# Attention stage rewritten: scores in fours into four banks, one shared bank used in written order, value sums normalised with VectorE's 32x32 transposes

## The reference, cut to what matters

```
q, k: 8 heads of 64;  v: 8 heads of 16           (xl = layernorm(x))
dots = q k^T / 8;  bias[h, i, j] depends on j - i only
attn = softmax(dots + bias);  out = (attn v) W_out + b_out;  x = x + out
```

## Time and profile before

| | us |
|---|---|
| median of 3 runs | 1186.83 (1186.79 to 1189.51) |
| profiled execution, its time | 1184.94 |
| its span | 1183.1 |
| one batch of attention (batches 1 to 6) | 56.63 |

### The profile page before, as it was taken

One profiled execution on the slowest core, in us unless ns is written; L12 is line 12 of the kernel. 1 busy time (PEld: TensorE's weight loads), 2 busy tenths in 40 slices (PEclk: granted clock), 3 DMA queues, 4 the chain that ended last, 5 costly groups with the idle time before them and its releaser, 6 DMA issues. The chain is left out here.

```text
span 1183.1 us, 23592 instructions
## 1 busy us (share of the span) xinstructions
PE 1072.6 (91%) x7860; PEld 794.2 (67%) x7860; DVE 895.0 (76%) x1941; ACT 831.8 (70%) x1727; POOL 515.3 (44%) x321
## 2 busy tenths in 40 slices
PE   3876499999999999989969999999999999997897
PEld 3442389899899899769954454545454555556897
DVE  7697988989889889747737586868686868675565
ACT  4897798898898988546636675757575757672565
POOL 0288788898998998635520001010101010011354
PEclk9898599999999999989989999999999999998999
DMA  3000355555785685233320000000000000002331
GB/s 95 4 2 9 86 142 139 138 146 150 189 254 165 175 228 159 75 112 104 110 61 28 1 2 19 1 19 2 19 1 19 1 19 10 10 19 60 102 98 50
DMA packets 107670, 89.50 MB, mean 76 GB/s; under 512 B 35703, under 2 KB 85628, under 8 KB 107552
## 3 DMA queue, kind: packets, MB, share of 16 engines
q1 hardware_dynamic: 98672, 66.01, 21.0%
q0 software_dynamic: 5568, 12.66, 3.0%
q10 hardware_dynamic: 3312, 9.33, 2.7%
HBM read 71.49 MB, written 17.39 MB: 75 GB/s over the span
## 5 line engine op out<-in xcount | busy, mean ns | idle before, releaser
L1041 DVE TENSOR_TENSOR_SCAN h<-d_a,p_dbu 128x1024 f32<-128x1024 f32 x128 | 289.5, 2278 | 31.5 <-ACT d_a L792 26.8
L738 POOL TENSOR_TENSOR h<-h,c_rep 128x1024 f32<-128x1024 f32 x126 | 295.1, 2368 | 27.2 <-DVE h L1041 26.1
L1369 POOL DMA_INDIRECT expert_rows<-r_row,r_dest x60 | 59.5, 991 | 468.4 <-DVEq L1264 453.7
L2017 ACT ACTIVATE arena<-arena,at_min 128x512 f32<-128x512 f32 x256 | 182.3, 720 | 96.4 <-DVE at_min L2127 93.7
L2127 DVE CUSTOM_DVE_ANT_0 arena<-at_p_scores,arena 128x512 f32<-128x512 f32 x256 | 174.2, 684 | 59.3 <-PE at_p_scores L1885 57.3
L792 ACT ACTIVATE d_a<-arena,a_exp 128x511 f32<-128x511 f32 x256 | 168.0, 710 | 19.1 <-DVE h L1041 19.0
L1892 PEld LDWEIGHTS at_p_probs_T<-ident,arena 128*128 128x128 f32 x1024 | 111.8, 141 | 91.8 <-issue 64.1
L1885 PE MATMUL at_p_scores<-arena,at_q_T 64*128 64x512 f32 x512 | 159.3, 641 | 1.5 <-DVE arena L2115 1.5
L1892 PE MATMUL at_p_probs_T<-ident,arena 128*128 128x128 f32 x1024 | 157.4, 281 | 1.8 <-ACT arena L2017 1.2
L931 PE MATMUL p_y_T<-ident,h 128*128 128x128 f32 x1024 | 132.5, 273 | 1.2 <-DVE h L1096 1.1
L784 ACT ACTIVATE b_du_T<-arena,b_T 128x256 f32<-128x256 f32 x304 | 128.8, 496 | 0.0
(11 more groups left out here) (263 smaller groups left out, 1618.0 us busy)
## 6 DMA issues: line engine op xcount, KB each, us to landing
c_rep<-c_rows SPq DMA_DIRECT2D x128, 256.0 KB, 3.6
diag_b<-diag_rows SPq DMA_DIRECT2D x52, 256.0 KB, 4.1
f_row<-expert_rows SPq DMA_DIRECT2D x78, 129.0 KB
arena<-in_w_all ACTq DMA_DIRECT2D x8, 578.0 KB, 5.4
arena<-bias_by_distance ACTq DMA_DIRECT2D x8, 448.0 KB, 5.0
x_tok<-in_x SPq DMA_DIRECT2D x4, 512.0 KB, 6.1
x_tok<-x_between SPq DMA_DIRECT2D x8, 256.0 KB, 2.7
diag_rows<-diag_b SPq DMA_DIRECT2D x4, 256.0 KB, 3.0
```

What stands on the lines that cost most here:

```text
L738: nc.gpsimd.tensor_tensor(h[:, n % HS, :, :], h[:, n % HS, :, :], cc, ALU.mult).then_inc(prod_done, 1)
L1041: nc.vector.tensor_tensor_scan(h[:, n % HS, :, :].rearrange("p c t -> p (c t)"), da[:, s % 2, :, :].rearrange("p c t -> p (c t)"), p_dbu[: ...
L2017: nc.scalar.activation(pr[:, slot, :], sc[:, slot, :], ACT.Exp, scale=-1.0, bias=mn[:, slot:slot + 1]).then_inc(probs_ready, 1)
```

## The change

- `psc` has four banks. Scores are issued in fours (`quad`), one quad ahead of its turns: heads alternate between the two halves of the array as before.
- A batch is 8 parts. In part p (n = 8b + p) TensorE does: quad n+1; half of a value sum (`values(n-2)`); slot A; turns 4n, 4n+1, 4n+2; slot B; turn 4n+3. VectorE does: `begin`, four biases, take 4n, take 4n+2, `extras`. ScalarE does: three exponentials, slot A's copy, the fourth, take 4n+1, slot B's copy, take 4n+3.
- `pmm` is one bank. The work in slots A and B uses it in written order; each waits for the reader of the one before. All copies of projections go to ScalarE, k1, k2, k3 and v too (but k0 and k1 of batch 0).
- The value sums are no longer copied, transposed back, normalised, transposed again and copied. VectorE transposes `pot` in 32x32 blocks, takes reciprocals, multiplies, and transposes in blocks again. W_out is spread over two zero-filled 128-row tables (8 small DMAs and a memset in expert layer 1), and the output takes 8 products in place of 4.
- The ring of probabilities has 7 tiles in place of 4. The prologue spreads batch 0's projections over all free banks.
- The router's stages, LayerNorm and the residual sum are lumped into `begin` and `extras`.

```diff
-        self.w_qk, self.w_v, self.w_o, self.b_o = k.take(2 * H * DQK), k.take(D), k.take(D), k.take(D)
+        self.w_qk, self.w_v, self.w_o, self.b_o = k.take(2 * H * DQK), k.take(D), k.take(2, D), k.take(D)
...
+        sp.wait_ge(self.filled, 3)
+        for hd in range(H):
+            gr, q = hd // 4, hd % 4
+            sp.dma_start(self.w_o[32 * q:32 * q + DV, gr, :], self.k.dram["w_o"][hd * DV:(hd + 1) * DV, :]
+                         ).then_inc(self.w_in, 16)
...
-        psc = k.ps("at_p_scores", [P, SCB, T], ctx=c)
+        psc = k.ps("at_p_scores", [P, 4, T], ctx=c)
-        pmm = k.ps("at_p_mm", [P, 2, T], ctx=c)
+        pmm = k.ps("at_p_mm", [P, T], ctx=c)
+        AT_A = {0: "X", 1: "k0", 2: "k1", 3: "q2", 4: "R", 5: "q3", 7: "V"}
+        AT_B = {0: "q0", 1: "q1", 2: "O", 3: "k2", 4: "L", 5: "N", 6: "k3"}
...
+            def output(b):
+                pe.wait_ge(normed, (b + 1) * NG)
+                for j in range(TPB):
+                    for gr in range(NG):
+                        mm = nc.tensor.matmul(pmm[:, j * P:(j + 1) * P], onT[gr][:, j * P:(j + 1) * P],
+                                              w_o[:, gr, :], start=gr == 0, stop=gr == NG - 1)
+                mm.then_inc(o_done, 1)
...
+            def quad(n):
...
+                for g in range(4 * n, 4 * n + 4):
+                    if g >= 4:
+                        pe.wait_ge(biased, g - 4 + 1)
...
+                    nc.tensor.matmul(psc[:, g % 4, :], qT[b % 2][half, hd // 2, it * P:(it + 1) * P],
+                                     kT[b % 2][half, hd // 2, :], start=True, stop=True).then_inc(scored, 1)
...
+            for n in range(B * QUADS):
+                b, part = divmod(n, QUADS)
+                if n + 1 < B * QUADS:
+                    quad(n + 1)
+                if n >= 2:
+                    values(n - 2)
+                slot(b, AT_A.get(part))
+                for g in range(4 * n, 4 * n + 3):
+                    turn(g)
+                slot(b, AT_B.get(part))
+                turn(4 * n + 3)
...
+            def norm(b, gr, parts):
+                n = b * NG + gr
+                if 0 in parts:
+                    dve.wait_ge(valued, 2 * n + 2)
+                    dve.wait_ge(norm_step, 2 * n)
+                    V.transpose(o_tok.rearrange("p n e -> p (n e)"), pot[:]).then_inc(pot_free, 1)
+                    dve.wait_ge(pot_free, n + 1)
+                    V.reciprocal(rden[:], o_tok[:, :, DV]).then_inc(norm_step, 1)
+                    dve.wait_ge(norm_step, 2 * n + 1)
+                    dve.wait_ge(normed, n)
+                    V.tensor_tensor(o_normed, o_tok, rden[:].unsqueeze(2).to_broadcast([P, T // 32, 32]),
+                                    ALU.mult).then_inc(norm_step, 1)
+                if 1 in parts:
+                    dve.wait_ge(norm_step, 2 * n + 2)
+                    if b > 0:
+                        dve.wait_ge(o_done, b)
+                    V.transpose(onT[gr], o_norm).then_inc(normed, 1)
+            def begin(b, part):
+                if b > 0 and part == 3:
+                    route(b - 1, 1, 2)
+                elif b > 0 and part == 6:
+                    route(b - 1, 8, 9, 10, 11)
+            def extras(b, part):
+                if part == 0 and b + 2 < B:
+                    stats_of(b + 2)
+                elif part == 1 and b > 0:
+                    norm(b - 1, 1, (0, 1))
+                elif part == 2 and b > 0:
+                    add(b - 1)
+                    route(b - 1, 0)
+                elif part == 3 and b > 0:
+                    route(b - 1, 3)
+                elif part == 4 and b > 0:
+                    route(b - 1, 4, 5, 6, 7)
+                elif part == 5:
+                    norm(b, 0, (0,))
+                elif part == 6:
+                    norm(b, 0, (1,))
+                elif part == 7 and b + 2 < B:
+                    normalise(b + 2)
+            for n in range(B * QUADS):
+                b, part = divmod(n, QUADS)
+                begin(b, part)
+                if n + 1 < B * QUADS:
+                    for g in range(4 * n + 4, 4 * n + 8):
+                        bias(g)
+                take(4 * n)
+                take(4 * n + 2)
+                extras(b, part)
```

More of the change, by code:

```diff
@@ L1898, in _, with values @@
[L1898 to L1912, removed]
+            def values(i):
+                vg, part = divmod(i, 2)
+                b = vg * VS // ST
+                hd0, gr, _, it = head_of(vg * VS)
+                if part == 0:
+                    for e in range(2):
+                        pe.wait_ge(turned_taken[e], (vg + 1) * (VS // 2))
+                    if vg % 2 == 0:
+                        pe.wait_ge(proj_taken, taken(b, "V"))
+                        if vg > 0:
+                            pe.wait_ge(pot_free, vg // 2)
+                for j in range(TPB // 2 * part, TPB // 2 * (part + 1)):
@@ L1952, in core @@
-            def core(b, par, first, last):
-                for s in range(ST):
-                    if s % 2 == 0 and s + 2 < ST:
-                        scores(b, par, s + 2)
-                    elif s % 2 == 0 and not last:
-                        scores(b + 1, 1 - par, s + 2 - ST)
-                    if s in VALUES_AT:
-                        values(b, par, *VALUES_AT[s])
-                    if not first:
-                        tail(b, par, s)
-                    elif s + LATE < ST:
-                        head(-1, s + LATE)
-                    turn(b, s)
-                    if not last:
-                        head(b, s)
@@ new lines, in _ @@
+            bank_free[0] = (proj_taken, taken(0, "V"))
+            for n in range(B * QUADS):
[9 more added lines that the diff above has]
+                turn(4 * n + 3)
+            for i in range(B * QUADS - 2, B * QUADS):
+                values(i)
@@ new lines, in _ @@
+            rstds(1, None)
+            take_projected(0, "q0", ppt[:, 0, :])
+            take_projected(0, "q1", pot[:])
+            for g, u, bank in ((0, "q2", pmm), (1, "k2", pot), (2, "q3", pmm), (3, "k3", pot)):
+                take_projected(0, u, bank[:])
+                exp(g)
+            take_projected(0, "V", pmm[:])
+            for n in range(B * QUADS):
+                b, part = divmod(n, QUADS)
+                more = n + 1 < B * QUADS
+                if more:
+                    for g in range(4 * n + 4, 4 * n + 7):
+                        exp(g)
+                slot(b, AT_A.get(part))
+                if more:
+                    exp(4 * n + 7)
+                take(4 * n + 1)
+                if part == 3:
+                    rstds(b + 2 if b + 2 < B else None, b - 1 if b > 0 else None) if b + 2 < B or b > 0 else None
+                elif part == 5 and b > 0:
+                    rt.act_exps(act, b - 1)
+                    rt.act_rows(act, b - 1)
+                slot(b, AT_B.get(part))
+                take(4 * n + 3)
@@ L2163, in core @@
-            def core(b, par, first, last):
-                for s in range(ST):
-                    bias(b, s)
-                    if s >= 2 and s % 2 == 0:
-                        take(b, s - 2)
-                    if not first:
-                        tail(b, s)
-                    elif s + LATE < ST:
-                        head(-1, 0, s + LATE)
-                    if not last:
-                        head(b, 1 - par, s)
-            for s in range(LATE):
-                head(-1, 0, s)
@@ new lines, in _ @@
+            stats_of(0)
+            normalise(0)
+            stats_of(1)
+            take_k(0, ppt[:, 1, :])
+            take_k(1, pmm[:])
+            for g in range(4):
+                bias(g)
+            normalise(1)
+            for n in range(B * QUADS):
+                b, part = divmod(n, QUADS)
+                begin(b, part)
+                if n + 1 < B * QUADS:
+                    for g in range(4 * n + 4, 4 * n + 8):
+                        bias(g)
+                take(4 * n)
+                take(4 * n + 2)
+                extras(b, part)
@@ L2185, in _ @@
+            dve.wait_ge(probs_ready, ALL)
+            plan.make_pad(dve)
+            norm(B - 1, 1, (0, 1))
+            add(B - 1)
+            route(B - 1, *range(0, 12))
+            plan.take_ends(dve)
             plan.dve(dve)
```

494 lines of the change are left out of this document (202 added, 292 removed).

## The result

| | before | after |
|---|---|---|
| median of the runs of one chip | 1186.81 (1185.79 to 1191.47, 10 runs) | 1195.74 (1192.77 to 1207.88, 10 runs) |
| ratio of the medians | | 1.0075, interval 1.0049 to 1.01 |
| profiled execution, time and span | 1184.94, 1183.1 | 1192.77, 1191.0 |
| first quad (pair) of batch 0 | 622.35 | 619.66 |
| first quad (pair) of the last batch | 1013.49 | 1019.31 |

The change made the kernel slower: 8.9 us. The direction of the forecast was wrong (1185.0, a hair faster); the time lies in its range. One of the ten runs after, 1207.88, stands apart, at a mean granted clock of 0.921 against 0.965 to 0.971 in the others.

What follows compares the result with a forecast made beforehand. TensorE was taken to bound attention, its savings given back in waits for VectorE: batches of 56.7 against 56.63, start and end included, -1.8 us, 1183.1 profiled, plus 1.9 for the median, 1185.0 us; range 1171 to 1199.

Steps and rivals of the forecast that it cites:

- 54.7 + 1.7 + 0.3 = 56.7: One attention batch: parts with their slots 54.7 us, plus VectorE work sticking out, 1.7 in part 6 and 0.3 in part 7.
- The quad: Four scores on TensorE: 1.92 us if the second pair follows without a gap, 2.12 if it does not; 1.92 taken.
- The block transpose: VectorE's transpose in the norm, shown by no row: taken as a PSUM copy, 0.69 us; dear end 1.2, cheap end 0.5.
- The wait at turn 4n+2: In every part TensorE stands 0.50 us until VectorE has copied turn 4n out of the bank.
- the holes for the extras: VectorE's free time before the next part's first bias: 2.6 us in part 1, 2.2 to 3.5 in parts 2, 3, 4, 0.
- the small stick-out of part 7: LayerNorm's products and one more on VectorE take 1.7 us in a hole of 1.35, so 0.3 sticks out.
- rival C: Slower: VectorE's work between parts 5 and 6 is longer than summed; with the transpose at 1.2, +10, 1195 us; chance 0.17.
- The start of batch 0's first quad: Batch 0's first projections follow each other, so the first quad starts at 619.2, 3.1 us earlier than before.
- eight projections 6.88 ... v 0.89: Work in a batch's slots on TensorE: projections 6.88, x 0.44, v 0.89, output 1.78, router 0.44 + 0.89 + 0.25, together 11.7 us.
- hands over in 0.05: The step from the end of VectorE's copy of turn 4n to turn 4n+2 takes 0.05 us.
- part 5 ... 1.7 us stick out: Half a norm and four router stages on VectorE, 2.8 us, exceed their hole; TensorE waits 1.7 us in part 6.
- TensorE's work, 50.2: TensorE's own work in one attention batch falls by 6.3 us to 50.2 us.

Runs made afterwards that it cites:

- the load in part 3: The changed kernel with one more VectorE reduction of 512 columns at the end of part 3's extras: 1199.79 us, one run.
- Swapped: The changed kernel with a turn's two waits exchanged, the bank's first and the exponential's second: 1196.0 us, ratio 1.006 to the kernel before.
- The experiment that moved the copy: The changed kernel with VectorE's copy of turn 4n put ahead of the four biases in part 6 alone: 1199.94 us, ratio 1.0076 to the kernel before.
- nine products: The changed kernel with 9 products that nobody reads in TensorE's gap of part 6: 1195.19 us, ratio 1.0041 to the kernel before.
- split burst: The changed kernel with the first half norm's reciprocal and product moved from part 5 to part 6: 1186.73 us, ratio 0.9975 to the kernel before.
- the pairs: The changed kernel with each quad issued as two pairs around the half value sum: 1209.99 us, one run.
- the other two edits: Norm's reciprocal and product moved to part 6 (1186.73 us alone), and a turn's two waits exchanged (1196.0 us alone), both on the changed kernel.
- moved everywhere with them: The changed kernel with slot B ahead of turn 4n+2 in every part, the norm's work moved and the waits exchanged: 1186.34 us, ratio 0.9975 to before.
- 1.44 (slot B): The changed kernel with slot B ahead of turn 4n+2 in every part, no other edit: 1191.92 us, ratio 1.0022 to the kernel before.
- the last version: The changed kernel with norm work moved, waits exchanged, slot B ahead of turn 4n+2 in parts 1, 4, 6: 1175.6 us, ratio 0.9896 to before.
- part 5 loaded: The changed kernel with one more VectorE reduction of 512 columns at the end of part 5's extras: 1211.28 us, one run.

## Why the prediction was wrong

The step that failed is the sum of a batch, "54.7 + 1.7 + 0.3 = 56.7". Its mechanism held, its sizes did not: a batch takes 57.63, a microsecond over the sum and no longer level with the 56.63 before. The terms too small were the product behind the value sums, the handing over of a bank, the burst ahead of part 6 and ScalarE's copy in part 7; and the fall of the clock, 1.5 us each, had been put at nothing.

*Right.* The quad: 1.92, as taken, in every chain. The Trainium skill's page "TensorE: Matmul & The Clock Gate", Part 3, "The mechanism", would in its strict form have given 2.12; the trace disagrees with that form. The block transpose: 0.706, as the copy that I took for it. The Trainium skill's page "VectorE: DVE Perf Modes", "The three transpose paths", led to an estimate near 0.7 or of 1.24, and the run decides for the first. The wait at turn 4n+2 in each part, the holes for the extras (the load in part 3 cost nothing), the small stick-out of part 7 (0.36 against 0.3, seen in part 0), and the way from the last turn to the residual sum (7.4 against 7.5) came as summed. The weights' small DMAs cost nothing, as taken: from the first to the last scatter of expert layer 1 there are 74.3 us, before 74.4. That VectorE's order between parts 5 and 6 sets part 6 was in the sum too, and it is rival C's place; but neither of its conditions was met. The transpose was not dear, and the burst was longer by 0.3, not by the 0.6 or more that C asked for. The loss of C's size (1195) came from several small terms, of which this is one.

*Right by luck, in part.* The start of batch 0's first quad, 619.66 against 619.2. The terms that the prediction gives (615.2, 3.5 and 0.9) add up to 619.6 and not 619.2. And both executions make their first projection at 615.19 only because the one after began to load x 1.5 earlier, at 606.00 against 607.46. It is 1.4 ahead already at the first scatter of expert layer 1 (527.8 against 529.2), so this lead comes from before anything that the change touches. From that load to the first quad the kernel after gains 1.2, not the 2.7 of the table. In the executions of the experiments, alike up to here, the first quad stands at 622.6 to 625.1.

*Wrong, with sizes.* By the last batch's first quad the kernel after is 5.8 us late, where I had 2.7 early. Measured: -2.7 at the start, +1.0 in batch 0 (52.33 against 51.34; I had it equal), 6 x 1.0, +1.5 for one clock fall. By the starts of TensorE's instructions the eight parts of a batch divide so (us; without a slot's share, the prediction's terms are 2.92, 1.44 and 1.03 a part, 5.39 where it wrote 5.38, and 2.0 for the bursts):

| | forecast | after | difference |
|---|---|---|---|
| quad's start to turn 4n | 28.6 | 29.2 | +0.6 |
| turn 4n to turn 4n+2 | 13.5 | 14.1 | +0.6 |
| turn 4n+2 to the next quad | 14.6 | 14.3 | -0.3 |

- **"eight projections 6.88 ... v 0.89"**. A projection or v in slot A stands behind the value sums and takes 0.10 more there than behind turns (0.96 and 1.00, for 0.86 and 0.89); x and the router's transposition take 0.05 more. This is the +0.6 of the first row, and the greater part of the 0.11 in parts 1 to 3 of the table of parts.
- **"hands over in 0.05"** was 0.14 (the chain above). The 0.05 came from VectorE to ScalarE; here it is TensorE that waits, at two semaphores in turn, the late one second. Swapped, it is 0.04, and each part 0.06 shorter: 0.5 a batch. Against the sum it shows as only 0.04 a part (turn 4n to 4n+2 is 1.475): the sum has 0.50 + 0.44 + 0.50 = 1.44 there, where its own working gave 1.40, and the copy starts at the lower end, 0.64 behind the turn.
- **"part 5 ... 1.7 us stick out"** was 2.0: part 6 is 0.28 longer than forecast. Where one waits for the one before, the pieces of the chain stand 0.02 to 0.17 apart; I had summed their lengths nearly without.
- **Part 7** is 0.25 longer: 0.10 for v behind the value sums, 0.04 from turn 4n to 4n+2, and 0.10 by the way that I called "0.1 late" for part 5 alone, ScalarE's copy of turn 4n+1 behind the fourth exponential: it ends at 909.85, and turn 4n+3 starts at 910.00. The experiment that moved the copy shows this way in part 6; for part 7 it is read from the timeline alone.
- **TensorE's work, 50.2**, is 51.85 busy in the trace. Where it stands anyway this costs nothing. Some 0.6 of it are the products behind the value sums; which other item of the 6.3 was too large was not tried.
- **The last batch** was 3.3 longer to its last turn than the 54.4 summed; about 1.5 of it is the second clock fall.
- **The clock.** I had named a lower clock only as a sign of being wrong and gave it no price. It takes 1.5 us of a batch that it hits. With gaps of 2.2 to 2.4 us (four executions) it hit one to three of the six middle batches and each time the last one. It accounts for 2 to 4 of the 8.9 us. Shown: filled (nine products) or shortened to 1.31 (split burst), the gap brings no fall, while everything else stays. Not shown: why it falls behind some of these equal gaps and not others, and from which length on. One fall came behind 1.77, six gaps of 1.91 (the pairs) brought none.

The account of one execution closes: -2.7 at the start (1.5 of it not the change's), 1.0 in batch 0, 6.0 in six batches, 1.5 for the fall in one of them, and 4.0 from the last batch's first quad to the residual sum (65.1 against 61.1, one fall in it) are 9.8, and the residual sum is 9.8 later. Of that, 2 us are gone by the end of the span (+7.9), in expert layer 2, which the change doesn't touch: it takes 106.6 us from there, before 108.5, and in the executions of the experiments 106.7 to 108.8, so this is a difference between executions. The execution after was the fastest of the ten, so the median may hold more falls than its two.

*The error in judgement.* The sum put the gain (TensorE 6 less) and the give-back (waits) at the same size, within 0.2 a batch. Every term left out was then a loss, since each was a wait on the path of the engine that had become late. A cancelling sum deserved a chance of slower above 0.37.

## What to carry to other kernels

When work is taken off the busiest engine, write down for each handoff which engine now answers last, and price the long in-order run of small instructions ahead of that answer with a gap between each two; here the place of two VectorE instructions (1.04 us) decided over 7 batches. A filler slot is worth trying part by part: moved everywhere it won in three parts and lost in two, used only where it won, with the other two edits, it made a batch of 55.2, where moved everywhere with them it made 56.2 to 56.8. A product's price depends on what stands before it, so take it from a row with the same neighbour. A gap of 2.4 us on TensorE can cost more than its length, so close or fill such a gap early.

## What the runs showed of the hardware

- The granted clock fell to half for 3.4 us behind an idle time of 2.35 us between stretches of dense work, in some batches and not in others with the same gap. At 1.2 GHz a turn took 1.09 for 0.63, a projection 1.71 (chain) for 0.86. In the versions whose longest gap in a middle batch was 1.91 (pairs), 1.44 (slot B), 1.31 (split burst) or 0.9 (the last version), one execution each, it never fell there; but it fell once behind 1.77, in batch 0 of the kernel with part 5 loaded.
- A semaphore wait that stands as an instruction of its own ahead of TensorE's transposes adds 0.10 to the handing over (0.14 against 0.04), if it is the one that ends last; net of a turn 0.03 longer, 0.06 a part.
- A projection takes 0.96 on TensorE behind the value sums and 0.86 behind turns, from its start to the next instruction's.
- VectorE's 32x32 block transpose of a 128x512 fp32 tile takes 0.71, out of PSUM as well as out of SBUF, like a copy.
- The releaser that a view names can mislead: the 2.35 gap is put down to ScalarE's exponential (L2003), which had long been done; the chain and the reordered copy show VectorE's biases and the copies behind them.
